# Transformer layer with attention and top-2 experts on one core: half of a projection issued earlier in the slot schedule, late ranks and scatters one to four slots later

## The reference

```python
x = x + layernorm(attention(layernorm(x)))      # 16 heads of 16, causal softmax, projections Wq, Wk, Wv, Wo
x = x + layernorm(ffn(layernorm(x)))            # router: softmax over 8 experts, the best two are kept
# ffn of a row: sum over its two experts of weight * (down(act(gate_up(row))) + bias), inner width 512
```

## Time and profile before

| | us |
|---|---|
| runs | 2085.91, 2081.51, 2084.46 |
| median | 2084.46 |
| the profiled execution, its own time | 2083.6 |
| its span in the trace | 2081.9 |
| TensorE busy (matmuls) | 1954.1 |
| VectorE busy | 1587.8 |
| ScalarE busy | 1335.3 |
| GpSimd busy | 939.8 |

### The profile page before, as it was taken

How to read it: one execution, slowest core, us unless ns; L and a number is a source line. 1 busy time by engine, 2 the same in 40 slices (tenths; PEclk the granted TensorE clock), 3 DMA queues, 4 the chain that set the end, 5 groups by cost and what they waited for, 6 DMA issues and landing times.

```text
span 2081.9 us, 50245 instructions
## 1 busy us (share of the span) xinstructions
PE 1954.1 (94%) x13588; PEld 1296.6 (62%) x13589; DVE 1587.8 (76%) x5419; ACT 1335.3 (64%) x3405; POOL 939.8 (45%) x1437
## 2 busy tenths in 40 slices
PE   6799999999999999999999889999999999999990
PEld 4344444444444444444433338999999999999990
DVE  2877788888888888888788836778777777777777
ACT  3377777777777777777777675555445454544446
POOL 5233344455655646556454554554333333333336
PEclk9799999999999999999999999999999999999995
DMA  7633546465454554644536457978988899998778
GB/s 209 190 113 121 180 142 206 149 181 182 141 177 145 164 164 140 191 130 153 167 120 208 132 175 226 263 226 242 272 255 260 262 264 261 263 258 256 231 225 326
DMA packets 259188, 414.81 MB, mean 199 GB/s; under 512 B 37040, under 2 KB 194992, under 8 KB 251824
## 3 DMA queue, kind: packets, MB, share of 16 engines
q1 hardware_dynamic: 219520, 368.19, 54.5%
q0 software_dynamic: 29680, 35.41, 9.6%
q10 hardware_dynamic: 9792, 8.93, 1.4%
HBM read 289.55 MB, written 122.28 MB: 198 GB/s over the span
## 4 chain that ended last, share of the span: by engine, by line
PE 84%; DVE 9%; issue 4%; ACT 1%; DMA 1%; SPq 1%; DVEq 1%; POOL 0%; ACTq 0%; POOLq 0%
PE ps_s L1469 17%; PE ps_o L1353 13%; PE ps_s L1315 12%; PE ps_e L1334 11%; PE ps_e L1469 6%; PE ps_o L1486 5%; PE ps_e L1486 5%; PE ps_w L1385 5%; PE ps_w L1400 3%; PE ps_w L1416 3%; DVE arena L747 2%; PE ps_e L1479 1%; DVE cmax L750 1%; PE ps_w L1440 1%; DVE space L127 1%
## 5 line engine op out<-in xcount | busy, mean ns | idle before, releaser
L1113 ACT ACTIVATE arena<-ps_e 128x512 f32<-128x512 f32 (+3 forms) x1536 | 687.2, 493 | 275.8 <-PE ps_e L1334 266.7
L747 DVE CUSTOM_DVE_ANT_0 arena<-ps_s,c 128x128 bf16<-128x128 f32 (+3 forms) x1024 | 479.2, 481 | 60.3 <-PE ps_s L1315 56.4
L1315 PE MATMUL ps_s<-arena 96*128 96x512 bf16 (+3 forms) x1536 | 488.5, 333 | 25.6 <-DMA arena<-qk_parts 7.1
L1334 PE MATMUL ps_e<-arena 98*128 98x512 bf16 (+3 forms) x1536 | 483.5, 329 | 3.0 <-ACT arena L1113 2.8
L750 DVE TENSOR_REDUCE cmax<-ps_s 128x1 f32<-128x512 f32 x512 | 351.3, 686 | 142.4 <-PE ps_s L1315 138.9
L1315 PEld LDWEIGHTS ps_s<-arena 96*128 96x128 bf16 x1536 | 151.8, 100 | 355.7 <-DVE cmax L747 91.7
L1353 PE MATMUL ps_o<-arena 128*32 128x512 f32 (+3 forms) x3072 | 329.3, 501 | 6.6 <-ACT ot L1127 3.5
L643 POOL TENSOR_SCALAR_AFFINE_SELECT arena<-arena 128x512 f32<-128x512 f32 x256 | 163.2, 637 | 295.4 <-ACT arena L1113 295.1
L627 POOL DMA_INDIRECT acc<-blank,place_now x135 | 215.5, 1596 | 129.6 <-POOL place_now L622 70.6
L1469 PE MATMUL ps_s<-arena 128*128 128x128 f32 x2192 | 269.4, 276 | 0.0
L1469 PEld LDWEIGHTS ps_s<-arena 128*128 128x128 f32 x2192 | 263.4, 193 | 5.5 <-ACT arena L1255 0.6
(11 more groups left out here) (184 smaller groups left out, 3045.0 us busy)
## 6 DMA issues: line engine op xcount, KB each, us to landing
arena<-in_gate_up SPq DMA_DIRECT2D x93, 1024.0 KB, 6.1
arena<-qk_parts SPq DMA_DIRECT2D x384, 128.0 KB, 2.9
c_h<-in_gate_up SPq DMA_DIRECT2D x46, 1024.0 KB
qk_parts<-space SPq DMA_DIRECT2D x120, 192.0 KB, 3.2
d_xin<-xs SPq DMA_DIRECT2D x140, 130.5 KB, 3.2
v_aug<-space SPq DMA_DIRECT2D x32, 512.0 KB, 4.9
arena<-v_aug SPq DMA_DIRECT2D x32, 512.0 KB, 5.1
o_t<-ot SPq DMA_DIRECT2D x64, 256.0 KB, 2.0
```

Of the source, the lines that this page charges most:

```text
L747: dve.tensor_tensor_reduce(summed[:, m % RJ, 0:w], ps_s[:, m % RS, 0:w], after[:, HALF - w:HALF], 1.0, LOWEST, ALU.add, ALU.max, dst).then ...
L1113: act.activation(pw[:, n % RP, 0:w], ps_e[:, n % RE, 0:w], ACT.Exp, scale=SCALE).then_inc(e_done, 1)
L1315: pe.matmul(ps_s[:, m % RS, 0:w], qs[0:ROWS, slot, i * P:(i + 1) * P], ks[0:ROWS, slot, k0:k0 + w], start=True, stop=True).then_inc(s_scor ...
L1334: pe.matmul(ps_e[:, n % RE, 0:w], ks[0:ROWS_M, slot, j * P:(j + 1) * P], qs[0:ROWS_M, slot, q0:q0 + w], start=True, stop=True).then_inc(e_ ...
```

## The change

For the pairs from the seventh on, steps 2 and 3 of the first product move from part 1 of slot A+2 to part 3 of slot A+1, the copy `first_part(a, 0)` from part 2 to part 0 of slot A+2, and the subtraction `remainder(a, 0)` from part 3 to part 1 of slot A+2. For groups 7, 8 and 9 `rank` and `place` move one slot later, for group 6 the third to eighth scatter move four slots later (from slots 380 to 385 to slots 384 to 389), and the scatters of groups 7 to 9, the late table and the clearing of ends one slot later. No instruction is added, removed or resized.

```diff
--- before.py
+++ after.py
@@ -183,16 +183,16 @@
     SCATTERS = [(n, k) for n, pairs in enumerate(GROUPS) for k in range(len(pairs) * 2 * TOPK)]
     STEADY = range(B - 2)
     EVEN = [30 + d for turn in range(0, 4 * NE, NE) for d in (turn, turn + 6, turn + 7, turn + 9, turn + 10)]
-    S_AT = [G_AT[n] + (30 + k if n == B - 3 else EVEN[k] if n in STEADY else 27 + k) for n, k in SCATTERS]
-    LATE_TABLE_AT = G_AT[-1] + 27
+    S_AT = [G_AT[n] + (30 + k if n == B - 3 else EVEN[k] if n in STEADY else 27 + (n > B - 2) + (k + 4 if n == B - 2 and k > 1 else k)) for n, k in SCATTERS]
+    LATE_TABLE_AT = G_AT[-1] + 28
     TABLE_AT, CLEAR_AT = G_AT[B - 3] + 29, max(S_AT) + 4
     TILE_AT = [NE * QUADS + 1 + 2 * n for n in range(BESIDE)]
     SLOTS = range(A_AT[0] - 6, TILE_AT[-1] + 2)
     MOMENTS = [(r, k) for slot, k, r in sorted((C_AT[r] + 3 + 6 * k, k, r) for r in range(PAIRS) for k in range(2))]
 
-    def groups_due(steady, late, slot):
-
-        return [n for n, start in enumerate(G_AT) if start + (steady if n in STEADY else late) == slot]
+    def groups_due(steady, late, slot, slack=0):
+
+        return [n for n, start in enumerate(G_AT) if start + (steady if n in STEADY else late + slack * (n > B - 2)) == slot]
 
     def rows_due(steady, quick, late, slot):
 
@@ -994,6 +994,8 @@
                     if s == 1:
                         for n in groups_due(22, 21, g):
                             choose(n, 1)
+                        for a in due(A_AT[FIRST_EVEN:], 2, g):
+                            remainder(FIRST_EVEN + a, 0)
                         for n in groups_due(27, NEVER, g):
                             place(n, 0)
                         for a in pairs_due(-6, -16, g):
@@ -1032,16 +1034,16 @@
                     if s == 2:
                         for n in groups_due(25, 22, g):
                             choose(n, 2)
-                        for n in groups_due(27, 24, g):
+                        for n in groups_due(27, 24, g, 1):
                             place(n, 1)
-                        for n in groups_due(28, 25, g):
+                        for n in groups_due(28, 25, g, 1):
                             place(n, 2)
-                        for n in groups_due(29, 26, g):
+                        for n in groups_due(29, 26, g, 1):
                             place(n, 3)
                     if s == 3:
-                        for n in groups_due(NEVER, 23, g):
+                        for n in groups_due(NEVER, 23, g, 1):
                             place(n, 0)
-                        for a in due(A_AT, 2, g):
+                        for a in due(A_AT[0:FIRST_EVEN], 2, g):
                             remainder(a, 0)
                         for a in due(A_AT, 4, g):
                             remainder(a, 1)
@@ -1177,6 +1179,9 @@
                     head, m = divmod((g - BEGIN) * 4 + s, NM)
                     if m == HIGH_AT and 1 <= head <= HEADS:
                         high(head - 1)
+                    if s == 0:
+                        for a in due(A_AT[FIRST_EVEN:], 2, g):
+                            first_part(FIRST_EVEN + a, 0)
                     if s == 1:
                         if 0 <= quad < QUADS and c == FIRST + 1:
                             head_out(quad, 0)
@@ -1526,8 +1531,11 @@
                             turn_rows(r)
                         for r in rows_due(16, 17, 17, g):
                             route(r, 1)
-                        for n in groups_due(NEVER, 23, g):
+                        for n in groups_due(NEVER, 23, g, 1):
                             rank(n)
+                    if s == 3:
+                        for a in due(A_AT[FIRST_EVEN:], 1, g):
+                            q_or_k(FIRST_EVEN + a, 0, (2, 3))
                     if s == 2:
                         for a in due(A_AT, 3, g):
                             q_or_k(a, 1, (0,))
```

## The result

| us | before | after |
|---|---|---|
| median of the runs | 2084.38 (2081.51 to 2085.91, 4 runs) | 2102.36 (2099.97 to 2102.59, 4 runs) |
| the profiled execution, its own time | 2083.6 | 2099.97 |
| its span | 2081.9 | 2098.3 |

The ratio is 1.0083, with a 95% interval of 1.0068 to 1.0098: slower by 18 us, where 2100 was forecast with a range of 2090 to 2108. All that follows compares profiled executions, +16.4 us of span.

A forecast was written before the change was run, and what follows sets the result against it. TensorE, busy 94%, was taken as the bound, with VectorE close behind. Pairs and the seventh pair +21.4 us, ranks -5.8, scatters zero: +15.6 us on 2083.6, 2099.2, median 2100 us, range 2090 to 2108.

The forecast's parts named there:

- Slot A+1: Slot gaining four matmul records on TensorE: 0.87 us added to 2.96, so 3.83 us, with no wait to pay for it.
- Slot A+2: Slot losing 0.92 us of TensorE work: still 2.87 us against 2.91, held by VectorE's reduction, subtraction and `mrow`.
- A pair: Slots A+1 and A+2 together: 5.87 to 6.70 us, +0.83 (bounds +0.52 and about +1.1); 25 pairs make 20.8 us.
- The scatters: Six scatters of group 6 and the rest moved a slot: zero for all, GpSimd being busy 45% overall.
- The seventh pair: Ahead of attention, where TensorE already waits 0.63 us for `mrow` before chunk 8: +0.6 us (0 to 0.9).
- The stop before values: TensorE's 0.45 us stop per pair, ended by VectorE's subtraction of the keys in A+4: stays, booked at zero.
- The ranks: Expert stage: stops of 2.31 and 1.87 us and 1.6 us of lower clock go, -5.8 us (low end -1.9).
- VectorE did not absorb the subtraction: Rival, 22%: chunk 8 in A+2 is not held, a pair costs +0.52; +7.2 us in all, 2092 us.
- ScalarE was not late with the copy: Rival, 6%: all three exponentials precede the copy in A+2, +1.3 us a pair; +27 us with the rest, 2111 us.
- TensorE kept nothing of its 0.92 us: Rival, 8%: A+2 shrinks by the full 0.92 us, the pair wins 0.05; -7 us with the ranks, 2077 us.
- The clock did not fall: Rival, 2%: short new TensorE stops in every pair each bring a lower-clock stretch, 1.6 us lost; 40 us, 2140.

The follow-up runs named there:

- product_only: Kernel before with only TensorE's two product steps moved to slot A+1, copy and subtraction left in place; 2099.46 us, ratio 1.0082.
- add_later: pair_only with GpSimd's addition of the residual (L692) one slot later; 2108.96 us, ratio 1.0129 to the kernel before.
- after_again: The changed kernel run once more, unedited, as a control; 2102.0 us, ratio 1.0087 to the kernel before.
- late_only: Kernel before with only the ranks, places, tables and scatters moved, products left as they were; 2077.34 us, ratio 0.997.
- keys_early: late_only with the keys' copy and subtraction one part earlier each, ahead of chunk 3 in slot A+4; 2059.65 us, ratio 0.9879 to the kernel before.
- pair_only: Changed kernel with ranks, places, tables and scatters left as before, only product, copy and subtraction moved; 2111.66 us, ratio 1.0125 to the kernel before.

## Why the prediction was right, and where not

- **Slot A+1**, forecast 3.83 us: 3.83.
- **Slot A+2**, forecast 2.87: 2.90. Chunk 7 at 1.18 and `max_rows` at 1.47 as in quad 26. The chain through copy, subtraction and `mrow` was right in its order and 0.03 us short in its length, by two errors that nearly cancel: the copy ended at 1.31 (542.95, forecast 1.37) and `mrow` began at 2.55 (forecast 2.63), but TensorE went on 0.15 us after its end and not 0.05. product_only shows its two parts, 0.53 and 0.32.
- **A pair**, forecast +0.83: +0.85. 25 of them make 21.3 us (20.8).
- **The five quads with `choose`**: not in the prediction, 5 x 0.59 = 3.0 us. The step that failed is the walk through VectorE's list, which was made on a pair without `choose`. And not its length alone: 0.49 of the 0.59 is an operation of GpSimd beside which VectorE could not work, as add_later shows. I had asked of every moved step what its engine runs next, and not what other engines run at that moment. The scatters and GpSimd were dismissed with its 45% busy share; a busy share says nothing of this.
- **The seventh pair**, forecast +0.6: its stop before chunk 8 went from 0.63 us to 1.10, +0.47.
- **The stop before values**, booked at zero: 0.45 us and 11.3 us in all, before and after.
- **The ranks**, forecast -5.8: the last stage became 5.05 us shorter in this profile, 5.5 in after_again and 4.4 in late_only. Timeline of TensorE at the two ranks, which answers to the earlier trace rows:

```profile
1325.10 0.18 PE L1457 MATMUL ps_w<-sel,c 128*128 128x40 bf16 x1
...
1378.72 0.19 PE L1457 MATMUL ps_w<-sel,c 128*128 128x40 bf16 x1 [0.43 <-ACT c_y L1228]
```

  The first stop is gone; of the second 0.43 us is left in this profile and nothing in those of late_only, after_again and keys_early, so half a tile of work just about covers ScalarE's copy. One stop that the forecast did not have, 0.83 us for `logits` at 1398 us before, is 0.16 after, and one of 0.31 at L1445 (1337 us) is new. The stops together give 2.31 + 1.44 + 0.67 - 0.31 = 4.1 of the 5.05 us. That leaves about 0.9 us for the stretch at the lower clock, booked at 1.6. The stop of 1.86 or 1.87 us at the second rank was followed by such a stretch in five of the seven profiles that have it, and not in pair_only and product_only, whose last stages (822.2 and 822.4) are hardly shorter than before's.
- **Quads 29 to 31**, booked at nothing, were 3.3 us shorter, and that was luck of one execution: after_again has 99.5. In large part it looks like the same thing as with `choose`. Timelines of VectorE in quad 29, first of after_again, then of after:

```profile
1216.48 2.06 DVE L880 TENSOR_TENSOR upto<-n_tiles,c 128x64 f32<-128x64 f32 x1
```

```profile
1216.62 0.22 DVE L880 TENSOR_TENSOR upto<-n_tiles,c 128x64 f32<-128x64 f32 x1
```

  And of GpSimd beside them, in the same order:

```profile
1215.56 1.01 POOL L702 DMA_INDIRECT xs<-c_h,slot_i  x1 [0.30 <-issue]
1216.58 0.64 POOL L643 TENSOR_SCALAR_AFFINE_SELECT arena<-arena 128x512 f32<-128x512 f32 x1
1217.19 1.26 POOL L671 TENSOR_TENSOR o_in<-o_in,rd_in 128x512 f32<-128x512 f32 x1
```

```profile
1214.99 1.00 POOL L702 DMA_INDIRECT xs<-c_h,slot_i  x1 [0.31 <-issue]
1216.91 0.64 POOL L643 TENSOR_SCALAR_AFFINE_SELECT arena<-arena 128x512 f32<-128x512 f32 x1 [0.92 <-ACT arena L1115]
```

  In after_again L880 began while GpSimd was in a row of three operations and ended with the last of them (1218.45), and TensorE stopped for 1.94 us at the next chunk; in after it came in a gap and took 0.22. The gap (0.92 us before L643, for an exponential) came with a lower clock on TensorE just before. Sums for the stretches at the lower level, first after, then after_again:

```profile
1213.30:1216.70 3.40, 3.40 (x16) 0.99 (x14) 2.91 (x9) 2.25 (x4) 2.37 (x4) 0.50 0.52 178
```

```profile
1221.00:1227.80 6.80, 6.76 (x29) 1.67 (x29) 5.22 (x21) 3.35 (x10) 4.59 (x9) 0.50 0.22 79
```

  So about two thirds of the difference of 2.9 us between these two profiles is the stop of 1.94, and the rest goes with 3.4 us less at the lower level. All this was read from the times, and not tried by moving anything. In add_later the meeting went a third way. VectorE and then GpSimd:

```profile
1212.39 0.64 DVE L880 TENSOR_TENSOR upto<-n_tiles,c 128x64 f32<-128x64 f32 x1
1212.96 1.88 DVE L882 TENSOR_SCALAR step<-n_tiles 128x8 f32<-128x8 f32 x1
```

```profile
1211.89 1.02 POOL L702 DMA_INDIRECT xs<-c_h,slot_i  x1 [0.17 <-issue]
1212.93 0.64 POOL L643 TENSOR_SCALAR_AFFINE_SELECT arena<-arena 128x512 f32<-128x512 f32 x1
1213.54 1.26 POOL L671 TENSOR_TENSOR o_in<-o_in,rd_in 128x512 f32<-128x512 f32 x1
```

  L880 ended 0.12 us after the first GpSimd operation, and it was L882, with one input, that stood until the end of the third (0.16 us in every other profile).

The profile's own sum: start +0.4, quads 0 to 24 +24.4, quads 25 to 28 0.0, quads 29 to 31 -3.35, the rest -5.05, which is +16.4. That it is so near the forecast of +15.6 is partly luck: 3.0 us missed for `choose` and 3.3 us of this one execution cancelled. The median has less of that luck. It grew by 18.0 us, 2.4 more than forecast, and the profiled execution was the fastest of its four; the span of after_again is 19.6 us above before's.

**The rivals.** VectorE did not absorb the subtraction (it would have been product_only's +0.53). ScalarE was not late with the copy. TensorE kept nothing of its 0.92 us: it got to chunk 7 sooner and waited. The clock did not fall: over 945 us with 50 new stops of about 0.3 us and five of 0.7 the granted clock is 1.00. The Trainium skill's rule on short idle times between matmuls ("TensorE: Matmul & The Clock Gate", section "A second HAM failure mode: psum-queue depth-cycling") would have had it swing; the traces of this stretch do not agree, and what is different here was not tried.

## What to carry to other kernels

When work is moved from one slot to another on an engine that is always busy, look at the second engine first: the slot that loses the work only gets shorter by the slack of whoever follows (here 0.35 of 0.92 us), while the slot that gains it gets longer by all of it. So take work off the leading engine only in a slot where the follower is ready early, and put the follower's own work where it is idle: the copy and subtraction of the keys, moved like that, won 24 us together with the late part. Walk the follower's list in every variant of the slot, and check what GpSimd is doing when a VectorE operation on SBUF, or GpSimd's own, comes to another time.

## What was not expected of the hardware

- A small VectorE operation with two SBUF inputs (L782) took 0.21 us alone and 0.70 and 1.13 us beside GpSimd's addition, and moving the addition away brought the 0.21 back. L880, of the same shape, took 0.22 us alone and 2.06 in a row of three GpSimd operations; in add_later it got through between the first and the second (0.64), and L882, with one SBUF input, took 1.88 us in place of 0.16. The reductions out of PSUM took their 0.69 (L750) and 0.28 us (L747) beside the same addition (before, 568.68 to 569.94).
- Quads that repeat hold their length to 0.01 us in nearly every profile, but one such meeting and the clock around it moved quads 29 to 31 of a profile by 3 us.
